# Two attention layers on one core: value product behind the scores, keys and values as plain fp32 products, two buffers of normalised rows, GpSimd's mask after the subtraction

## What is computed

```python
# layer 0 (cosine), x: (64, 64, 256), 16 heads of 64, one key and one value head
xn = ln(x, g_norm)
q  = (xn @ Wq).reshape(b, n, 16, 64)
k, v = split(xn @ Wkv)                      # 64 + 64 columns, plus one null key and value
q, k = l2norm(q) * q_scale, l2norm(k) * k_scale
sim  = einsum('bhid,bjd->bhij', q, k) * 8 + attn_bias        # causal and key mask
out  = einsum('bhij,bjd->bhid', softmax(sim), v)
c    = ln(out @ Wout, g_out)
x    = x + spikes(relu(c @ W_fc.T) ** 2 @ W_proj.T)
# layer 1: the same attention without the l2 norms (q * 1/8), another bias and mask,
# then a block with a small attention and a mixture of 8 experts (top 2) and a shared one
x    = x + moe_block(attention1(x))
```

## Time and profile before

| | before |
|---|---|
| median of 3 runs (lowest to highest) | 1524.06 us (1522.95 to 1525.0) |
| profiled execution, first to last instruction | 1465.9 us, mean granted TensorE clock 0.967 |
| median less that span | 58.2 us |
| PE busy | 1342.3 us (92%) |
| DVE busy | 1123.4 us (77%) |
| ACT busy | 892.0 us (61%) |
| POOL busy | 793.0 us (54%) |

### The profile page before, as it was taken

How to read it: one execution, slowest core, us unless ns; L and a number is a source line. 1 busy time by engine, 2 the same in 40 slices (tenths; PEclk the granted TensorE clock), 3 DMA queues, 4 the chain that set the end, 5 groups by cost and what they waited for, 6 DMA issues and landing times.

```text
span 1465.9 us, 43550 instructions
## 1 busy us (share of the span) xinstructions
PE 1342.3 (92%) x15663; PEld 1176.4 (80%) x15664; DVE 1123.4 (77%) x2225; ACT 892.0 (61%) x2229; POOL 793.0 (54%) x836
## 2 busy tenths in 40 slices
PE   4799999999889999889999999878998888999993
PEld 4788988888679999778888888667886667888882
DVE  4798888888845565789999999878885797554557
ACT  3567767776556666646566665557775545555556
POOL 2556656665535454456555564578884005777740
PEclk9799999999999999989999999999997999999996
DMA  8200000000130000000000000010003203333318
GB/s 227 53 7 8 10 8 8 8 10 9 34 81 5 1 0 0 3 9 8 9 9 8 10 7 9 27 53 15 14 14 117 94 2 119 103 101 98 97 41 341
DMA packets 79895, 65.09 MB, mean 44 GB/s; under 512 B 48878, under 2 KB 73457, under 8 KB 78706
## 3 DMA queue, kind: packets, MB, share of 16 engines
...
...
## 4 chain that ended last, share of the span: by engine, by line
PE 77%; DVE 10%; issue 5%; ACT 4%; POOL 2%; DMA 1%; SPq 0%; DVEq 0%; ACTq 0%; POOLq 0%
PE psQ L1957 13%; PE psW L2050 12%; PE psQ L2352 8%; PE psW L2331 5%; PE psS L2075 4%; PE psS L2024 4%; PE psT L1986 3%; PE psQ L2153 3%; PE psS L2153 3%; PE psW L2141 3%; PE psM L2141 3%; PE psM L2011 3%; PE psT L2320 1%; PE psM L1975 1%; PE psT L2339 1%
## 5 line engine op out<-in xcount | busy, mean ns | idle before, releaser
L742 POOL TENSOR_TENSOR pn<-ex,rden 128x1024 f32<-128x1024 f32 x64 | 143.8, 2247 | 234.1 <-PE psT L1986 211.7
L1957 PEld LDWEIGHTS psQ<-xT,wq 128*128 128x128 f32 x1536 | 202.8, 202 | 46.3 <-issue 24.2
L1957 PE MATMUL psQ<-xT,wq 128*128 128x256 f32 x1536 | 222.9, 299 | 1.7 <-ACT cur L1067 1.5
L2050 PE MATMUL psW<-wout,oT 128*128 128x256 f32 x1536 | 208.2, 291 | 7.0 <-ACT oT L976 4.8
L2050 PEld LDWEIGHTS psW<-wout,oT 128*128 128x128 f32 x1536 | 193.2, 192 | 13.2 <-ACT oT L976 7.5
L2352 PE MATMUL psQ<-W,exT 128*128 (+1 forms) x624 | 172.6, 412 | 0.0
L782 POOL TENSOR_TENSOR hT<-hf,hT 128x512 fp32r<-128x512 f32 x64 | 85.8, 1340 | 99.4 <-ACT hT L1063 99.2
L862 POOL DMA_INDIRECT rows<-xf,src x72 | 73.1, 1016 | 108.7 <-DVE src L1839 83.4
L2352 PEld LDWEIGHTS psQ<-W,exT 128*128 128x128 f32 x624 | 111.3, 192 | 18.9
L2331 PE MATMUL psW<-W,ehT 128*128 (+1 forms) x624 | 102.7, 301 | 8.3 <-DVE ehT L1869 8.2
L925 ACT ACTIVATE qT<-psQ 128x512 f32<-128x512 f32 x128 | 76.6, 598 | 52.9 <-PE psQ L1957 50.9
...
...
## 6 DMA issues: line engine op xcount, KB each, us to landing
...
vv<-vp SPq DMA_DIRECT2D x256, 16.0 KB, 1.8
...
bvv<-v_all SPq DMA_DIRECT2D x128, 16.0 KB, 1.8
rows<-xf,src POOLq DMA_INDIRECT x72
```

Of the source, the lines that this page charges most:

```text
L742: nc.gpsimd.tensor_tensor(pn[:], ex[t % 2][:, :, 0:S], rden[:].unsqueeze(2).to_broadcast([P, H, S]), ALU.mult).then_inc(sem("t_pn"), 1)
L1957: mm = nc.tensor.matmul(psQ[:, cc, h * QT:h * QT + QT], wq[w][:, k, c * P:c * P + P], xT[g % 2][u][:, k, :], start=(k == 0 and j == 0), st ...
L2050: mm = nc.tensor.matmul(psW[:, 0:D], oT[u][:, c, :], wout[w][:, c, :], start=(u == 0 and c == 0 and w == 0), stop=(u == 1 and c == CH - 1))
```

## The change

1. PE makes the value product of tile i-3 at the end of step i, behind the scores of tile i-1, and puts it into `psT` in place of `psS`; before, step i made that of tile i-4 between the two query banks. The turn of the probabilities goes from the head of the step (tile i-4) to behind the turn of `xn` (tile i-3). `psS` holds only scores now. ACT and DVE take the output of the value product at the head of the next step, before everything else of ACT and before the scores on DVE.
2. Keys and values are one plain fp32 product: the stationary operand is an unrounded copy `xfull` of the turned rows (three buffers, the third in two halves, written by ACT), the moving one is `wkvn` in fp32. Two matmuls in the program take the place of six. It is made behind the first query bank, not before it. DVE no longer makes the remainder of `wkvn`.
3. `pn` has two buffers: POOL waits for the turn of the tile before the last one.
4. In layer 1 POOL makes the masked bias after DVE's subtraction (`t_sub`), behind the root; before, right behind `pn` (`t_sum`).
5. In layer 0 DVE takes the scores out of PSUM before it makes the null column. In the last steps `oT` of tile 30 is made earlier, behind `O` and ahead of the last exponential on ACT.

```diff
-        pn = sb("work", "pn", [P, H, S], F32)
+        pn = [sb("work", f"pn{i}", [P, H, S], F32) for i in range(2)]
...
-                        reach(pool, sem("t_pTp"), done + t)
-                        nc.gpsimd.tensor_tensor(pn[:], ex[t % 2][:, :, 0:S], rden[:].unsqueeze(2).to_broadcast([P, H, S]),
+                        reach(pool, sem("t_pTp"), done + t - 1)
+                        nc.gpsimd.tensor_tensor(pn[t % 2][:], ex[t % 2][:, :, 0:S], rden[:].unsqueeze(2).to_broadcast([P, H, S]),
...
+                    if not L["cosine"]:
+                        norm_root(done, i + 4)
...
-                        reach(pool, sem("t_sum"), done + t)
+                        if t:
+                            pool.wait_ge(sem("t_sub"), done + t)
...
+                def output_hi(t):
+
+                    if live(t):
+                        reach(act, sem("t_wo"), done + t)
+                        act.wait_ge(sem("t_pv"), done + t + 1)
+                        for b in range(2):
+                            nc.scalar.activation(oT[0][:, :, b * S:b * S + S], psT[:, b, :].rearrange("p (c q) -> p c q", q=S),
+                                                 ACT.Identity, bias=nvcol[:, 0:1]).then_inc(sem("t_ohi"), 1)
...
                 def step(i):
+                    if not i == TILES + 2:
+                        output_hi(i - LATE)
...
+                    reach(act, sem("t_kvp"), done + t - XFULL + 1)
+                    if t % XFULL < 2:
+                        nc.scalar.activation(xfull[t % XFULL][:], x_bank(t).rearrange("p (k q) -> p k q", q=P), ACT.Copy)
...
-                    if not TILES < i:
-                        probabilities_turned(i - LATE)
+                    query_bank(i, 0)
                     t = i
                     if live(t):
...
                         for k in range(KD):
-                            for j, (u, w) in enumerate(PASSES):
-                                mm = nc.tensor.matmul(psM[:, 0:KVN], xT[g % 2][u][:, k, at], wkvn[w][:, k, :],
-                                                      start=(k == 0 and j == 0), stop=(k == KD - 1 and j == 2))
+                            mm = nc.tensor.matmul(psM[:, 0:KVN], xfull[2][k][:] if t % XFULL == 2 else xfull[t % XFULL][:, k, :], wkvn[:, k, :],
+                                                  start=(k == 0), stop=(k == KD - 1))
                         mm.then_inc(sem("t_kvp"), 1)
-                    query_bank(i, 0)
...
                     norm_transpose(done, i + 3)
-                    if TILES <= i:
-                        probabilities_turned(i + 1 - LATE)
+                    probabilities_turned(i - TURNED)
...
-                        reach(pe, sem("t_olo"), 2 * (done + i - LATE + 1) if i >= LATE else 0)
                         reach(pe, sem("t_left"), done + t)
...
+                    t = i - TURNED
+                    if live(t):
+                        pe.wait_ge(sem("t_pT"), done + t + 1)
...
+                                mm = nc.tensor.matmul(psT[f, b, :], vv[t % VV][slot, b, :], pT[slot, :, b * S:b * S + S],
+                                                      start=True, stop=True, skip_group_check=True)
+                        mm.then_inc(sem("t_pv"), 1)
```

114 lines of the change are left out of this document (53 added, 61 removed).

## The result

Same chip, four runs each: the kernel before 1523.51 us (1522.68 to 1525.0), the changed one 1499.15 (1496.8 to 1501.65), ratio 0.9843, 95% interval [0.9825, 0.9862]. That is 24.4 us, against the 24.5 of the prediction.

The account below looks back on a forecast made before the run. PE's own work was taken to set both layers' periods, with DVE right behind in layer 1. Terms 11.0 + 6.5 + 3.4 - 2.4 + 6 = 24.5 us saved gave a median of 1499.6 us, range 1490 to 1510.

Parts of the forecast that it names:

- Term 1: Keys and values on PE: four plain fp32 records instead of six matmuls save 0.22 us a step, 11.0 us.
- Term 2: Value product behind the scores: one pair of edges into and out of array quarters goes, 0.13 us a step, 6.5 us.
- Term 3: Layer 1 output product: its wait for DVE's `oT` goes, 0.14 us a step, 3.4 us.
- Term 4: Layer 1 keys and values: new wait for `kT` behind ACT's `oT` evictions costs 0.1 us a step, 2.4 us, at most 3.6.
- Term 5: First steps: 6 of 13.6 us of PE's waits before value products and keys and values go.
- Term 6: Last steps: value product one step earlier, last exponential waits behind two evictions on ACT; nothing, give or take 3 us.
- 58.2 us outside the span: Amount by which the runs' median exceeds the profiled span of 1465.9 us, assumed to stay after the change.
- (a): Layer 1 stays near 10.2 us a step through another chain, needing 0.4 us of new wait: 1509 us, chance 0.17.
- (b): The plain product for keys and values costs 0.96 us, its upper bound: 1523.6 us, no change, chance 0.04.
- (c): Layer 1: POOL gets ahead of DVE at `xn` and `vp`, DVE stands still, 1545 us, slower, chance 0.05.

Follow-up runs that it names:

- fp32 alone: Kernel before with only the plain fp32 product for keys and values (and its full-precision row copies): 1472.9 us against 1468.5, ratio 1.004.
- two pn alone: Kernel before with only two buffers of normalised rows: 1529.6 us against 1527.1, ratio 1.002.
- three products: Changed kernel with keys and values again from split halves in three fp32r products, their new place kept: 1453.4 us against 1468.1 before, ratio 0.9901.
- kT first: Changed kernel with ACT copying the turned keys `kT` ahead of `oT` in each step: 1450.8 us against 1468.1 before, ratio 0.9879.
- after again: Changed kernel, unchanged, run on another chip: 1444.1 us against 1469.5 before, ratio 0.9841.
- before again: Kernel before, unchanged, profiled once more: 1466.3 us, one run.
- combined: Changed kernel with `kT` ahead of `oT` in layer 1 only, reordered last steps, DVE's second feed-forward weight split moved later: 1427.8 us against 1469.5 before.

## Why the prediction came out right, point by point

**What bounds the kernel.** "PE's own work sets both periods" was wrong for layer 1. There 0.31 us less work on PE (fp32 alone) left the step at 10.19, and taking `pn` from beside the null column shortened it to 10.07 and 9.84: it was a loop through DVE, closed by the 0.14 us wait inside the output product. For layer 0 it was right as far as the runs go, by a small margin: with 1.3 us of standing still on DVE (two pn alone) a step took 11.43. The row with PE busy for 244.61 of 244.61 us hides that wait, because the ends of matmuls are modelled.

**Term 1, the plain product: 0.22 a step, 11.0 us.** Measured in the new order 0.16 and 0.23 a step, 9.3 us by the medians and 10.7 with each beside its own before. The seams moved both sides of it: the new place alone takes the six records from 0.70 to 240.31 - 239.68 = 0.63, the four take 237.73 - 237.34 = 0.39 instead of the 0.48 that I had counted, and the bank behind them 1.55 instead of 1.48. The price read from L2098 was good enough, 0.122 from record to record for a forecast of 0.12. Its half clock was an inference, though: the view's granted clock from 18.9 to 20.6 us is 1.00, and what speaks for half speed is that query records are 0.21 apart up to 18.9 us and 0.12 from 20.8 on. Nor do the runs show that two cycles a column set the price, since the six fp32r records, at 0.105 to 0.117 each, are hardly closer. The Trainium skill's four passes for true fp32 (FP8 and Floating Point Precision, TensorE Precision Notes), by which eight would stand against six and the edit would lose, don't give the time of this shape: the measured row decides. The failed step is another: the term was added as if it stood by itself. Alone, in the order of before, the edit costs 4.4 us.

**Term 2, one pair of edges: 0.13 a step, 6.5 us.** The pair of edges was sized well, the move was not. In layer 0 value product and squares take 248.86 - 247.02 = 1.84 in three products, 1.01 + 1.01 in before: 0.18, and in layer 1 scores and value product 1.95 for 2.10: 0.15. But a step of layer 0 fell by 0.44 with the move alone. The rest is at other seams, where I had counted nothing: turn of the keys and first bank 1.60 for 1.74, keys and values and second bank 2.11 for 2.24, turn of the probabilities 0.79 for 0.86, less 0.08 at the turn of `xn`. Why each seam is shorter was not tested. Since keys and values are still behind the first query bank in three products, this surplus is that of the whole new order and not of the value product's place. "The turn of the probabilities costs the same wherever it stands" was wrong by this 0.07.

**Term 3, DVE's `oT` in layer 1: 0.14 a step, 3.4 us.** The wait is gone (727.31 - 724.30 = 3.01 us) and the value product's move removes it by itself, since `oT` leaves the loop. "It pays by taking the 1.65 and 0.54 us of standing still out of DVE's loop" is the failed step for parts 3 and 4: DVE does lose them, and in the steady steps of the new order PE doesn't wait for DVE. In the order of before the second buffer gives layer 1 0.12 a step and costs layer 0 0.22.

**Term 4, the new wait for `kT`: -0.1 a step, at most 3.6 us.** The place and the cause were right, the size was not. `kT` ends 721.21 - 719.48 = 1.73 behind the turn of the keys, a little before the 1.8 that I counted. But I compared it with the start of the matmul, at 1.74, and what needs `kT` first is the weight load, which in kT first begins at 1.48. Between after again and kT first it is 0.27 a step, some 7 us over the 26 steps of layer 1, twice my bound. A wait is to be counted from the weight load that it holds up.

**Term 5, the first steps: 6 us.** 8.1 us in layer 0 (57.24 in before again, 49.17 in after again) and 1.4 in layer 1. The kernel with the move alone has the 8.1 too, and nothing of the 1.4 (44.99 us for 44.83); where that comes from was not tested.

**Term 6, the last steps: 0, give or take 3.** The largest miss, 8.4 and 8.1 us lost in the result's traces, 8.4 and 5.7 between before again and after again. I had seen the exponential behind two evictions and priced it at nothing. In the last steps each engine's order is a chain with no next tile to fill it, so its waits add: 3.1 us on DVE, 2.75 on ACT, 0.9 beside the weight split, and the lower clock around PE's pauses, which on the output products alone is about half of the loss. In the combined kernel 7.2 us of it are back in layer 0 and 3.6 in layer 1, beside after again.

So 24.5 was hit by luck: the move, worth more than I had it, met two losses that I had at a third of their size or at none. By stretches, before again less after again, the steady steps gave 27.7 us where the sum had 18.5, the first steps 9.5 for 6, the last steps -14.1 for 0, and all the rest 1.4 for 0. By edits what is left adds up: 15.6 us for the move with both losses inside, 9.3 to 10.7 for the product on top of it, nothing for the other parts, 24.9 to 26.3 beside the 25.4 measured. The sum's 58.2 us outside the span were the other error that cost nothing: the median was forecast as a difference, and the difference hardly depends on the chip (24.4 and 25.4 us).

**The rivals.** (a) A chain of ACT's `oT`, `kT`, then keys and values: it is there, with 0.27 us a step instead of 0.4. (b) The four records take 0.39, not 0.96. (c) DVE was first at both places: `xn` took 0.33 us as a rule (at most 1.38), `vp` 0.22. But the exclusion behind it, the Trainium skill's rule (SBUF — State Buffer, Who interferes with whom), did decide something. In the order of before it is what holds layer 1's loop, and by the rows of layer 0 it made the fp32 product alone and the two buffers alone slower. And the trace agrees with its condition of two SBUF inputs: in the new layer 0 `pn` runs beside `oT` and the read of the scores, which each have an input in PSUM, and they take 1.41 and 1.22 us as they do without it.
